# Order of the products in the first two gate quads of each token half, in a recurrent layer with a ternary feed-forward on eight cores

## The reference, cut to what matters

```
xi, z = split(x @ Win.T)                       # 2 x 2048 channels
lam   = exp(-8 softplus(omega) * sigmoid(xi @ Wl.T + bl))
v     = xi @ Wv.T + bv
# a scan over the tokens: a Householder reflection by v, then the gate
h = lam * (h - 2 v (v.h)/(v.v)) + (1 - lam) * xi
y = layernorm(x + (silu(z) * h) @ Wout.T)
out = layernorm(y + int8_like(y) @ (ternary - 1).T + b)
```

## Time and profile before

| | |
|---|---|
| median of 3 runs | 2442.48 us (2439.76 to 2479.71) |
| the profiled execution | 2450.9 us |
| its span on the slowest core (core 6) | 2449.3 us |
| spans of the 8 cores | 2424.2 to 2449.3 us |
| mean granted TensorE clock of the cores | 0.990 to 0.996 |
| matmul busy share | 97% |
| VectorE, ScalarE busy share | 64%, 31% |

### The profile page before, as it was taken

The page is one execution under the profiler, slowest core; times in us unless marked ns, Lnnn a source line. Parts: engine busy times, 40 slices in busy tenths (PEclk is TensorE's granted clock), DMA queues, the critical chain, the costliest instruction groups (busy, mean ns, idle before and its releaser), DMA issues.

```text
span 2449.3 us, 32720 instructions; the slowest of 8 cores (2424.2 to 2449.3 us)
## 1 busy us (share of the span) xinstructions
PE 2366.2 (97%) x11153; PEld 1205.6 (49%) x11370; DVE 1569.7 (64%) x1988; ACT 760.2 (31%) x1034; POOL 2.3 (0%) x7
## 2 busy tenths in 40 slices
PE   7999999999999999999998999999999999999997
PEld 3555555545554444444443444444445555555553
DVE  5666766576614556665654465556655878888887
ACT  6545455455422321333330232212223121211221
POOL 0000000000000000000000000000000000000000
PEclk9999999999999999999999999999999999999999
DMA  6778788999997687677789887776678974444430
GB/s 174 241 232 270 255 270 246 282 279 300 302 303 235 201 236 214 204 218 232 213 217 299 250 245 215 219 217 189 193 209 245 289 244 166 172 167 161 172 138 35
DMA packets 319333, 548.11 MB, mean 224 GB/s; under 512 B 16832, under 2 KB 148416, under 8 KB 306112
## 3 DMA queue, kind: packets, MB, share of 16 engines
q1 hardware_dynamic: 319168, 546.01, 73.6%
HBM read 338.32 MB, written 207.62 MB: 223 GB/s over the span
## 4 chain that ended last, share of the span: by engine, by line
PE 72%; DMA 8%; DVE 8%; issue 4%; SPq 4%; ACT 3%; DVEq 0%; ACTq 0%
PE pb L177 71%; DMA wcs<-CO 4%; SPq L203 4%; DVE CO L206 2%; DMA XRAW<-x_fm 1%; DVE TS L206 1%; ACT CO L200 1%; DVE OUT L1082 1%; DMA XC<-xcs 1%; DMA zs<-ZOUT 1%; DMA xcs<-CO 1%; ACT ZOUT L200 1%; ACT WB L200 0%; DVE Y L1029 0%; DVE STT L1019 0%
## 5 line engine op out<-in xcount | busy, mean ns | idle before, releaser
L177 PE MATMUL pb<-XC,WC 128*128 128x512 bf16 x5268 | 1161.3, 380 | 24.8 <-DMA WC<-wcs 13.3
L177 PEld LDWEIGHTS pb<-XC,WC 128*128 128x128 bf16 x5376 | 526.6, 98 | 656.3 <-issue 28.5
L177 PE MATMUL pb<-XB,WB 128*128 128x512 bf16 x1988 | 486.6, 384 | 3.4
L177 PE MATMUL pb<-XH,WH 128*128 128x512 f32 x1024 | 332.2, 445 | 26.1 <-ACT XH L200 16.9
L177 PE MATMUL pb<-WO,GHL 128*128 128x512 bf16 x1488 | 347.9, 379 | 3.4 <-ACT GHL L200 0.6
L177 PEld LDWEIGHTS pb<-XB,WB 128*128 128x128 bf16 x2048 | 180.9, 99 | 255.7 <-issue 77.8
L177 PEld LDWEIGHTS pb<-XH,WH 128*128 128x128 f32 x1024 | 195.1, 191 | 90.9 <-issue 33.8
L177 PEld LDWEIGHTS pb<-WO,GHL 128*128 128x128 bf16 x1536 | 149.8, 99 | 148.7 <-issue 0.9
L541 DVE SCALAR_TENSOR_TENSOR GPS<-pb,COLS,GPS 128x512 f32<-128x512 f32 x64 | 48.0, 751 | 256.1 <-PE pb L177 256.1
L200 ACT ACTIVATE CO<-TS 128x512 bf16<-128x512 f32 (+1 forms) x200 | 143.0, 717 | 165.8 <-DVE TS L206 150.0
L206 DVE TENSOR_TENSOR CO<-TS,CO 128x512 bf16<-128x512 f32 (+1 forms) x200 | 158.6, 793 | 25.5 <-ACT CO L200 25.1
(11 more groups left out here) (123 smaller groups left out, 1782.1 us busy)
## 6 DMA issues: line engine op xcount, KB each, us to landing
WC<-wcs SPq DMA_DIRECT2D x224, 512.0 KB, 5.5
wcs<-CO SPq DMA_DIRECT2D x224, 256.0 KB, 7.1
xcs<-CO SPq DMA_DIRECT2D x56, 512.0 KB, 5.3
XC<-xcs SPq DMA_DIRECT2D x28, 1024.0 KB, 15.7
xfs<-XF SPq DMA_DIRECT2D x16, 1024.0 KB, 5.1
GRAW<-w_l SPq DMA_DIRECT2D x32, 512.0 KB, 9.4
GRAW<-w_v SPq DMA_DIRECT2D x32, 512.0 KB, 9.0
zs<-ZOUT SPq DMA_DIRECT2D x16, 1024.0 KB, 11.7
```

Of the source, the lines that this page charges most:

```text
L177: return q.do("tensor", lambda e: e.matmul(out, lhsT, rhs, start=start, stop=stop), waits, inc)
```

## The change

It orders the products of quads (0, 1) and of quads (16, 17) in turn: (0,0), (1,0), (0,1), (1,1) and so on to (0,6), (1,6). All other quads run as before. `ORDER` holds the order, `GIDX` the place of a product in it; ring slot, bank and `load_wc` go by that place.

- The loads of the sums of xi come one per two products: m 1 and 2 before the stage, m 3 to 6 after places 0, 2, 4 and 6; for the second half `load_xc(1, k)` after place 105 + 2k. Quad 15 is at places 105 to 111, the pair (16, 17) at 112 to 125.
- Within a pair, `forget` of the gate quad is called at its m 5 and 6 with p 1 finished after the last product of the pair, and there also both "m" stores with the loads of z, and both `values`. The stores k, g, a of the pair are issued at m 4 and 5 of the quad that follows (before: at m 1 and 3).
- The stores of quad 15: "a" of p 0 after its last product, "a" of p 1 after (16,0), "k" and "g" after (16,2) and (16,3). Before: all three at (16,3) and (16,5).
- The 24 preparations of later weights skip quads 15 to 17 instead of 15 and 16, and end one quad later.

```diff
+    PAIRED = (0, 1, NQ // 2, NQ // 2 + 1)
+    ORDER = []
+    for q0 in range(0, NQ, 2):
+        pair = [(q0 + k, m) for k in range(2) for m in range(7)]
+        ORDER += sorted(pair, key=lambda qm: qm[::-1]) if q0 in PAIRED else pair
+    GIDX = {qm: g for g, qm in enumerate(ORDER)}
+    XCAT = {2 * k: (0, 3 + k) for k in range(4)}
+    XCAT.update({7 * (NQ // 2 - 1) + 2 * k: (1, k) for k in range(7)})
...
-        return (7 * qi + m) % 8 if qi < NQ - 1 else (1, 2, 3, 4, 5, 1, 4)[m]
+        return GIDX[qi, m] % 8 if qi < NQ - 1 else (1, 2, 3, 4, 5, 1, 4)[m]
...
-    for m in range(1, 4):
+    for m in range(1, 3):
         for part in range(2):
             load_xc(0, m, part)
...
-    PREP = {qi: k for k, qi in enumerate([qi for qi in range(2, 28) if qi not in (15, 16)])}
+    PREP = {qi: k for k, qi in enumerate([qi for qi in range(2, 29) if qi not in (15, 16, 17)])}
+    for g, (qi, m) in enumerate(ORDER):
...
+        if g + RING < 7 * NQ:
+            load_wc(g + RING)
+        if g in XCAT:
+            load_xc(*XCAT[g], 0)
+            load_xc(*XCAT[g], 1)
+        if not final or m < 6:
+            evac_quad(qi, m)
...
+        if kind == 0 and qi and not paired:
+            if qi - 1 in PAIRED:
+                if m in (4, 5):
+                    put("gka", m - 4, qi - 1)
+            elif m in (1, 3):
+                put("kga", m // 2, qi - 1)
+        if kind == 0 and m in (4, 5):
+            load_xn(qi, m - 4)
+        if kind and not final and not paired and m in (2, 4):
+            put("m", m // 2 - 1, qi - 1)
+            load_z(qi, m // 2 - 1)
+        if kind and not final and not paired and m >= 5:
+            finish(values(qi, m - 5))
+        if kind == 0 and m >= 5:
+            gates[m - 5] = forget(qi, m - 5, 2 if qi == NQ - 2 and m == 6 else 1)
+            next(gates[m - 5])
+            if m == 6:
+                finish(gates[0])
+                if qi == NQ - 2:
+                    for _ in range(5):
+                        next(gates[1])
+                elif not paired:
+                    finish(gates[1])
+        if kind and paired and m == 6:
+            finish(gates[1])
+            for p in range(2):
+                put("m", p, qi - 1)
+                load_z(qi, p)
+            for p in range(2):
+                finish(values(qi, p))
+        if qi == NQ // 2 - 1 and m == 6:
+            put("a", 0, qi)
+        if qi == NQ // 2 and m == 0:
+            put("a", 1, qi - 1)
+        if qi == NQ // 2 and m in (2, 3):
+            put("kg", m - 2, qi - 1)
```

More of the change, by code:

```diff
@@ L480, in load_wc @@
     def load_wc(g):
-        qi, m = divmod(g, 7)
+        qi, m = ORDER[g]
         h, jc, kind = QUADS[qi]
@@ L494, in mm_prod @@
         h, jc, kind = QUADS[qi]
-        g = 7 * qi + m
+        g = GIDX[qi, m]
         wt, xt = WC[g % RING], XC[m]
@@ L548, in evac_quad @@
         if m == 0:
-            t = t_dst["a"] = first(c21, c11)
+            t = t_dst[qi, "a"] = first(c21, c11)
         elif m == 1:
-            t = t_dst["b"] = first(c12, c22)
+            t = t_dst[qi, "b"] = first(c12, c22)
         elif m == 2:
-            t_dst["c"] = tt(c11, ps, c11, AL.add, (tok, t_dst["a"]))
-            t = t_dst["d"] = tt(c22, ps, c22, AL.add, (tok, t_dst["b"]))
+            t_dst[qi, "c"] = tt(c11, ps, c11, AL.add, (tok, t_dst[qi, "a"]))
+            t = t_dst[qi, "d"] = tt(c22, ps, c22, AL.add, (tok, t_dst[qi, "b"]))
         elif m == 3:
-            t_dst["e"] = last(c12, b0, (t_dst["b"],))
-            t = t_dst["c"] = tt(c11, c11, ps, AL.subtract, (tok, t_dst["c"]))
+            t_dst[qi, "e"] = last(c12, b0, (t_dst[qi, "b"],))
+            t = t_dst[qi, "c"] = tt(c11, c11, ps, AL.subtract, (tok, t_dst[qi, "c"]))
         elif m == 4:
-            t_dst["f"] = last(c21, b1, (t_dst["a"],))
-            t = t_dst["d"] = tt(c22, c22, ps, AL.subtract, (tok, t_dst["d"]))
+            t_dst[qi, "f"] = last(c21, b1, (t_dst[qi, "a"],))
+            t = t_dst[qi, "d"] = tt(c22, c22, ps, AL.subtract, (tok, t_dst[qi, "d"]))
         elif m == 5:
-            t = last(c11, b0, (t_dst["c"],))
-            t_dst[qi, 0] = (t_dst["e"], t)
-        else:
-            t = last(c22, b1, (t_dst["d"],))
-            t_dst[qi, 1] = (t_dst["f"], t)
+            t = last(c11, b0, (t_dst[qi, "c"],))
+            t_dst[qi, 0] = (t_dst[qi, "e"], t)
+        else:
+            t = last(c22, b1, (t_dst[qi, "d"],))
+            t_dst[qi, 1] = (t_dst[qi, "f"], t)
         free[b] = (t,)
@@ L1151, in build @@
     gates = [None, None]
-    PREP = {qi: k for k, qi in enumerate([qi for qi in range(2, 28) if qi not in (15, 16)])}
-    for qi, (h, jc, kind) in enumerate(QUADS):
+    PREP = {qi: k for k, qi in enumerate([qi for qi in range(2, 29) if qi not in (15, 16, 17)])}
+    for g, (qi, m) in enumerate(ORDER):
+        h, jc, kind = QUADS[qi]
         final = qi == NQ - 1
[L1155 to L1215, removed]
@@ new lines, in build @@
+        paired = qi in PAIRED
+        mm_prod(qi, m, last_hooks if final else None)
+        if final and m == 0:
+            load_c("K", 0, tuple(t_gall[0]) + (t_xcmm[0],))
+            load_c("A", 0, (t_wcmm[7 * NQ - 7],))
+        if g + RING < 7 * NQ:
[5 more added lines that the diff above has]
+            evac_quad(qi, m)
+        k = PREP.get(qi)
+        if k is not None and m == 2:
+            if k:
+                prep_store(k - 1)
+            else:
+                prep_load(0, (t_in_pe,) + t_gr_free[1])
@@ new lines, in build @@
+        if k is not None and m == 4:
+            prep_split(k, (t_in_pe,) + t_gr_free[1] if k == 0 else ())
+        if k is not None and m == 6 and k + 1 < NIC + NDC:
+            prep_load(k + 1)
+        if qi == 29 and m == 2:
+            prep_store(NIC + NDC - 1)
+        if kind == 0 and qi and not paired:
[4 more added lines that the diff above has]
+                put("kga", m // 2, qi - 1)
@@ new lines, in build @@
+        if kind and paired and m == 6:
[11 more added lines that the diff above has]
+            put("kg", m - 2, qi - 1)
+        if final and m == 1:
+            load_c("M", 0, (t_xcmm[1],))
+            load_c("Z", 0, (t_xcmm[1],))
@@ L1216, in build @@
+        if final and m == 2:
+            load_c("A", 1, (t_xcmm[2],))
+            load_z(qi, 0)
+        if final and m == 3:
+            load_z(qi, 1)
+        if final and m >= 3:
+            for ic in range(4):
+                load_wo(4 * (m - 3) + ic)
     t_in_gates = t_quad[NQ - 1, 6]
```

## The result

The changed kernel takes 2419.66 us, median of 20 runs, where the kernel before takes 2438.69 us in its 20; the ratio of the undisturbed runs is 0.993, with a 95% interval of 0.9914 to 0.9946. That is 17 us less (0.007 x 2438.7) by the ratio and 19.0 by the two medians; it is under 1%, but clear of the noise. The prediction was 2421 us and 21.4 us less; its range, 2411 to 2438, holds the time. On a second chip the two stood at 2422.1 and 2439.7 us, ratio 0.9928 (0.9913 to 0.9943).

A forecast was written before the change was run, and what follows sets the result against it. TensorE was taken as the bound, with 24.4 us lost beside it. Gains of 6.7 us at the start and 14.7 in the middle, 21.4 together, took the 2442.5 us median to 2421 us, range 2411 to 2438 (8 in 10).

The forecast's parts named there:

- What bounds: Whole kernel: TensorE bounds it, matmuls filling 97% of the span; reordering returns at most what TensorE loses beside it.
- The ceiling: Gate stage: 24.4 us lost by TensorE in two stretches, 1.0% of the time, the most the change could gain.
- The start: Gate stage, 722.9 to 800 us: waits for XC lose 6.7 us, all forecast to go; bounds 4.6 to 6.7.
- The middle: Gate stage, 1280 to 1375 us: ring loads queued behind XC lose 17.7 us; 14.7 us forecast to be gained.
- The stall that is left: Middle, around places 123 to 126: late ring load still costs 3 us, of 0 to 4.7.
- the first rival: Middle: queue rate nearer 0.278 MB/us, no stall left, 24.4 us gained, 2418 us; chance 0.27.
- The rate: Middle, SyncE's queue: loads land at 0.257 to 0.278 MB/us, the lower taken as nearer.
- What is moved: Ends of pairs and later stores: moved work is covered, nothing added to the time; bound 0 to 4 us in the middle.
- All of it goes: Start and middle: no stall remains, the full 24.4 us is gained, 2418 us; chance 0.27.
- The DMAs stay the bound in the middle: Middle: stores among loads press the rate to 0.235 MB/us; load 14.4 us late, gain 10 us, 2432 us; chance 0.15.
- SyncE held: End of a pair: ring loads wait behind the "m" store; some 19 us lost in the middle, 2445 us; chance 0.05.
- It doesn't do what it says: SyncE's queue: XC was not what overloads it, so the time stays at 2442 us; chance 0.03.

The follow-up runs named there:

- the two halves: Changed kernel with only quads 0 and 1, or only 16 and 17, in turn; against the kernel before, ratios 0.9982 and 0.9957.
- More bytes: Changed kernel plus four 1 MB memory-to-memory copies in SyncE's queue after places 107, 109, 111 and 113: 2438.3 us, 20.3 more.

## Why the prediction was right, and where it was off

- **What bounds.** Right: TensorE has the same work, and the gain is the loss beside it. The ceiling, 24.4 us, was right for the execution it was read from; as the usual loss of the kernel it was mis-sized. That execution lost 24.1 us in the mean of its cores, two later ones 18.1. The prediction knew that its execution lay 8.4 us above the median that it had, and took the whole sum over to the median as if the stalls had no part in that. Nor are they all of it: core 6 took 2449.3 us, 17.4 more than the late cores of the two later traces in the mean, and 8.7 of them came before the gate stage, 5.1 in it and 3.6 in the output stage.
- **The start.** Right in kind: the waits went entirely, on every undisturbed core of every trace with that pair. Measured for it alone 4.4 us (2.0 to 6.8, from the interval), for 6.7 predicted; its loss in the kernels with the old start varied from 2.7 to 10.7 us by core.
- **The middle.** Right in mechanism, shown by the loads issued early (15 us back with the products still in turn) and by their removal (13.7 us gained, nothing lost in the middle). The mis-sized term is again the ceiling: 17.7 us was core 6 of one trace, where the mean was 15.4 there and 12.9 later.
- **The stall that is left.** The prediction took 3 us; 0 to 1.9 us was left, 1 us or more on 4 of the 20 undisturbed cores of its three traces. So what came is nearer to the first rival's picture than to the forecast's 1 to 6 us. The place, product 124, was right on core 6. Two slips stand in the working. The load issued at 1341.28 follows place 112 and is used at place 118, so it is due at 67.3 us and not at 62.2; the check on the kernel before then gives 13.8 and 8.0 us rather than 18.9 and 13.1, and neither rate explains the 17.7. The row at 1358.71 is the start of that product, so the load landed 17.4 us after its issue and not 14.1: 26.0 + 17.4 - 25.9 = 17.5 us of stall, which is the whole loss, and 19.5 / 79.3 = 0.246 MB/us. And the 26.5 MB of the change hold the ring's load of place 105, which the 19.5 MB of before leave out; without it the load after 119 comes 2.8 us late at 0.257, not 4.7.
- **The rate.** Counted alike, from the first XC load to the end of a wait, it was 0.246 MB/us on core 6 of the first trace, 0.254 to 0.263 on its other cores, 0.262 to 0.270 in the two later ones, and 24.5 / (1360.72 - 1267.42) = 0.263 in the changed kernel. With 0.246 for both kernels the working would have left 7.3 us of stall. That a small one was forecast is in part luck: the wrong landing time made the rate of core 6 look like that of the others.
- **The number.** 2421 for 2419.66 us is closer than the working deserves. The median of three runs before was 3.8 us too high (2442.5 for 2438.7) and the gain 2.4 to 4.4 us too large, and the two cancel. Within the gain the ceiling was some 6 us too high and the stall left some 2 us, which cancel in part as well.
- **What is moved.** Right: no loss shows at the tail of a pair. The load of GNC, for which a landing 3.4 us after the pair's end was counted, was there 3 us before it. VectorE waited 1.16 us for it, where before it had waited 15.33 (in order of time, core 6, beside the earlier trace rows):

```profile
1368.15 1.23 DVE L614 SCALAR_TENSOR_TENSOR GNC<-GLS,GNC 128x1024 f32<-128x1024 f32 x1 [1.16 <-DMA GNC<-xfs]
```

  and so the "m" store of p 1 went out 18 us after the pair's end and not 25. The bound of 0 to 4 us was at its lower end.
- **The rivals.** "All of it goes" is nearly what happened, with a smaller all. "The DMAs stay the bound in the middle" is a matter of a few us of margin: 2 MB of stores issued 5 or 6 places early bring back 4.6 us. "SyncE held" is real: in the one amount tried, 21.2 us of VectorE work, all of it beyond some 3.3 us of cover became idle time, and the change became a loss. "It doesn't do what it says" is excluded by the two halves and by the loads issued early.
- **The limit that the Trainium skill gives**, about 358 GB/s for one core of a pair ("DMA: Bandwidth & Descriptors", Specifications): the mean over the busy stretch doesn't reach it. The DMA share was 1.00 at 296 GB/s, and leaving that figure out of the sum was right.

## What to carry to other kernels

Where all loads go through one queue in order, a stall for a small steady load can be the work of a large one in front of it. Sum the bytes issued against the time, with the rate of that stretch, and compare each landing with its due time; what counts is when the large loads are issued, and an order of the work that lets them be issued later is worth having even if it computes the same. And take the size of a stall from more than one execution, and from more than one core: here the same two stalls were 15.4 to 28.1 us.

## What the runs showed of the hardware

- The rate at a full DMA share (0.96 to 1.01 from 1270 to 1365 us) differed with the mix: 279 to 302 GB/s on the undisturbed cores with loads and stores, 257 to 276 GB/s with four copies from memory to memory among them.
- A DMA's issue on SyncE took 0.42 us in the median between 900 and 1200 us, and single ones took up to 9.4 us with the DMA share near 1.00 (17.1 with the copies of "More bytes"). A ring load issued there landed after 10.7 us in the median in the changed kernel and 14.1 before, where over the whole kernel it took 5.5.
- The cores start the gate stage (their first weight load that reads XC) at two times, 7 to 18 us apart: of each two cores (0, 1), (2, 3), (4, 5) and (6, 7) one is late, and not always the same one. In the first trace of before cores 0, 2, 4 and 6 (715.8 to 722.7 us) are late and the others start at 703.0 to 706.1; after the change cores 1, 2, 5 and 6 are late (712.8 to 717.5). The slowest undisturbed core of every trace is a late one. What makes a core late was not tried.
